# One transfer per piece over all partitions, and three lows made by accumulating DMAs, in a gather and interaction tower

## What is computed

```python
# e: (512, 39, 16), gathered by ids from 39 tables; x0 = xk = e
for W, b in ((w0, b0), (w1, b1), (w2, b2)):         # 128 outputs each
    z = relu(einsum('bhd,bkd,hks->bsd', x0, xk, W) + b)
    xk, direct = z[:, :64], z[:, 64:]               # the last layer: all of z is direct
logit = concat(direct).sum(-1)                      # (512, 256)
h = relu(concat([logit, dense_ctx]) @ W_top1 + b_top1)
h = relu(h @ W_top2 + b_top2)
y = h @ W_top3
```

## Time and profile before

| | us |
|---|---|
| median of 3 runs | 657.21 |
| the runs | 656.03 to 660.27 |
| the profiled execution | 660.38 |
| its span | 658.6 |

### The profile page before, as it was taken

One profiled execution on the slowest core, in us unless ns is written; L12 is line 12 of the kernel. 1 busy time (PEld: TensorE's weight loads), 2 busy tenths in 40 slices (PEclk: granted clock), 3 DMA queues, 4 the chain that ended last, 5 costly groups with the idle time before them and its releaser, 6 DMA issues.

```text
span 658.6 us, 6385 instructions
## 1 busy us (share of the span) xinstructions
PE 613.0 (93%) x1996; PEld 378.3 (57%) x1996; DVE 546.7 (83%) x616; ACT 410.6 (62%) x553; POOL 536.2 (81%) x325
## 2 busy tenths in 40 slices
PE   0169899999999999999999999999999999999998
PEld 0026465666656566656666666666566666655563
DVE  1248699898989898998989898989989898969740
ACT  2025857676676758576766757586777667575622
POOL 6657899898989899998989998999989886747520
PEclk9998899999999999999999999999999999999899
DMA  6689794938374756749384747567494847420000
GB/s 220 136 191 187 160 172 98 180 73 184 89 147 109 139 104 132 148 101 179 71 165 107 146 100 140 114 126 154 95 180 75 162 110 134 96 46 1 0 0 0
DMA packets 53216, 78.60 MB, mean 119 GB/s; under 512 B 39081, under 2 KB 42025, under 8 KB 49891
## 3 DMA queue, kind: packets, MB, share of 16 engines
q1 hardware_dynamic: 47566, 75.11, 54.9%
q0 software_dynamic: 5120, 1.29, 2.0%
q10 hardware_dynamic: 496, 1.80, 1.1%
HBM read 76.23 MB, written 1.94 MB: 119 GB/s over the span
## 4 chain that ended last, share of the span: by engine, by line
PE 38%; POOL 38%; ACT 11%; issue 6%; DMA 4%; DVE 3%; SPq 1%; DVEq 0%; ACTq 0%
POOL low L361 29%; PE z L681 20%; PE z L698 9%; POOL gat L351 9%; ACT x L448 7%; PE z L713 6%; ACT high L428 2%; DMA spread<-x_rows 2%; DVE prod L591 2%; DMA gat<-table_dram,index 2%; ACT r L472 1%; DMA x_rows<-gat 1%; DVE base L626 1%; DVE low L634 1%; PE base L758 1%
## 5 line engine op out<-in xcount | busy, mean ns | idle before, releaser
L361 POOL TENSOR_TENSOR low<-prod,high 128x1024 fp32r<-128x1024 f32 (+2 forms) x160 | 380.7, 2399 | 58.8 <-ACT high L428 57.7
L591 DVE TENSOR_TENSOR prod<-spread,x 128x1024 f32<-128x1024 f32 (+1 forms) x256 | 307.6, 1212 | 38.7 <-ACT x L448 37.7
L681 PE MATMUL z<-prod,w_sb 128*128 128x512 f32 (+3 forms) x608 | 294.0, 604 | 36.9 <-DVE prod L572 32.4
L428 ACT ACTIVATE high<-prod 128x1024 fp32r<-128x1024 f32 (+2 forms) x160 | 167.7, 1058 | 116.9 <-DVE prod L591 98.4
L698 PE MATMUL z<-high,high_w_L 128*128 128x512 f32 (+1 forms) x448 | 205.9, 459 | 1.0 <-ACT high L438 1.0
L713 PE MATMUL z<-low,high_w_L 128*128 128x512 f32 (+1 forms) x448 | 182.6, 488 | 5.5 <-POOL low L361 3.5
L681 PEld LDWEIGHTS z<-prod,w_sb 128*128 128x128 f32 (+3 forms) x608 | 116.2, 192 | 124.0 <-issue 101.6
L351 POOL DMA_INDIRECT gat<-table_dram,index x160 | 154.7, 967 | 37.0 <-issue 35.3
L698 PE MATMUL z<-high,low_w_L 128*128 128x512 f32 (+1 forms) x448 | 179.0, 400 | 0.0
L448 ACT ACTIVATE x<-z,bias_sb 64x512 f32<-64x512 f32 (+1 forms) x186 | 120.2, 646 | 15.1 <-PE z L681 7.4
L713 PEld LDWEIGHTS z<-low,high_w_L 128*128 128x128 f32 (+1 forms) x448 | 82.8, 190 | 71.7 <-issue 45.8
(11 more groups left out here) (37 smaller groups left out, 62.4 us busy)
## 6 DMA issues: line engine op xcount, KB each, us to landing
spread<-x_rows SPq DMA_DIRECT2D x139, 192.0 KB, 13.5
spread<-x_rows SPq DMA_DIRECT2D x30, 546.0 KB
spread<-x_rows SPq DMA_DIRECT2D x47, 256.0 KB, 4.2
spread<-x_rows SPq DMA_DIRECT2D x15, 468.0 KB
x0base<-x_rows SPq DMA_DIRECT2D x47, 78.0 KB
gat<-table_dram,index POOLq DMA_INDIRECT x160, 5.6
x_rows<-gat SPq DMA_DIRECT2D x16, 72.0 KB, 2.2
wt_sb<-wt_dram SPq DMA_DIRECT2D x2, 512.0 KB, 19.0
```

Source lines behind the costliest of these rows:

```text
L361: pool.tensor_tensor(low[0:rows, h, 0:k, :], prod[0:rows, slot(c, kind, g), 0:k, :], high[0:rows, h, 0:k, :].bitcast(F32), ALU.subtract).t ...
L428: act.activation(high[0:rows, split_slot(c, kind, g), 0:k, :], prod[0:rows, slot(c, kind, g), 0:k, :], ACT.Copy).then_inc(high_ready, 1)
L591: dve.tensor_tensor(prod[0:rows, slot(c, kind, g), :, :], spread[0:rows, c % 2, g, :].unsqueeze(1).to_broadcast([rows, k, N]), x[0:rows, : ...
L681: last = pe.matmul(z[:, :], w[0:rows, at + j, :], prod[0:rows, slot(c, kind, g), j, :], start=g == 0 and j == 0, stop=closes and j == k - 1)
```

## The change

Three things are changed.

**Loads.** `load_base` and `load_spread0` issue one DMA over 117 partitions instead of three over 39, and `load_spread` one over 128 partitions for each piece instead of four over 32; the source is given as three blocks of 39 rows, or as four blocks whose row is read 32 times. ACT issues none any more. `ROWS` grows, so that the last rows that are read exist.

**Lows by DMA.** For L2 group 0 and L1 groups 1 and 5 (`BY_DMA`) ACT writes the high with its sign turned, the weights that go with it are turned as well, and a DMA of POOL's queue adds the product onto the high, in place, once PE has summed the high (`add_low`). What stands there then is the low; PE multiplies it by an unturned copy of the high weights (`plus_w`) four groups later (`DMA_PLACES`), or at the end of the stage. POOL's subtraction for these three groups goes. The rings become nine, six and four (`RING`, `HRING`, `LRING`).

**Dense weights.** They lie in `spread0` and are loaded at the end of SP's list, after L0 of the last chunk.

```diff
+ROWS = F + FPT * (-(-max(DPT * T0 - 1, FPT * -(-F // FPT) - F) // FPT))
-RING = 8
-HRING = 4
+RING = 9
+HRING = 6
+LRING = 4
+BY_DMA = (("L2", 0), ("L1", 1), ("L1", 5))
+ADD_PLACES = 1
+DMA_PLACES = 4
...
-                for j in js:
-                    sp.dma_start(x0base[j * F:(j + 1) * F, :], bass.AP(row.tensor, row.offset, [[N, F], [1, N]])
-                                 ).then_inc(base_in, 16)
+                sp.dma_start(x0base[:, :], bass.AP(row.tensor, row.offset, [[0, DPT], [N, F], [1, N]])
+                             ).then_inc(base_in, 16)
...
-                for j in js:
-                    many = min(end, DELTAS - j * T0) - at
-                    row = x0_dram[c, j * T0 + at:j * T0 + at + 1, 0:1]
-                    src = bass.AP(row.tensor, row.offset, [[N, F], [1, many * N]])
-                    sp.dma_start(spread0[j * F:(j + 1) * F, at:at + many, :].rearrange("p t n -> p (t n)"), src
-                                 ).then_inc(done, 16)
+                row = x0_dram[c, at:at + 1, 0:1]
+                src = bass.AP(row.tensor, row.offset, [[T0 * N, DPT], [N, F], [1, (end - at) * N]])
+                sp.dma_start(spread0[0:R0, at:end, :].rearrange("p t n -> p (t n)"), src).then_inc(done, 16)
...
-                for q in qs:
-                    many = min(end, F - q * G1) - at
-                    row = x0_dram[c, q * G1 + at:q * G1 + at + 1, 0:1]
-                    src = bass.AP(row.tensor, row.offset, [[0, QUAD], [1, many * N]])
-                    sp.dma_start(spread[q * QUAD:(q + 1) * QUAD, c % 2, at:at + many, :].rearrange("p g n -> p (g n)"),
-                                 src).then_inc(spread_in[p][c % 2], 16)
+                row = x0_dram[c, at:at + 1, 0:1]
+                src = bass.AP(row.tensor, row.offset, [[G1 * N, FPT], [0, QUAD], [1, (end - at) * N]])
+                sp.dma_start(spread[:, c % 2, at:end, :].rearrange("p g n -> p (g n)"), src
+                             ).then_inc(spread_in[p][c % 2], 16)
...
+            sp.wait_ge(prod_done, PROD_NUMBER[NCH - 1, "L0", G0 - 1])
+            sp.dma_start(wt1_sb, wt1[0:2 * P, :].rearrange("(t p) n -> p t n", p=P)).then_inc(top_in, 16)
...
+            def add_low(c, kind, g):
+
+                n = BY_DMA.index((kind, g))
+                pool.wait_ge(high_summed[n], c + 1)
+                rows, k = shape_of(kind, g)
+                pool.dma_start(high[0:rows, split_slot(c, kind, g), 0:k, :].rearrange("p k n -> p (k n)"),
+                               prod[0:rows, slot(c, kind, g), 0:k, :].rearrange("p k n -> p (k n)"), accum_op=ALU.add
+                               ).then_inc(dma_low[n], 16)
...
+                        for f in gs:
+                            if (kind, f) in BY_DMA and f + ADD_PLACES == g:
+                                add_low(c, kind, f)
...
-            act.wait_ge(base_in, 16 * DPT * (c + 1))
+            act.wait_ge(base_in, 16 * (c + 1))
...
-                               prod[0:rows, slot(c, kind, g), 0:k, :], ACT.Copy).then_inc(high_ready, 1)
+                               prod[0:rows, slot(c, kind, g), 0:k, :], ACT.Copy,
+                               scale=-1.0 if (kind, g) in BY_DMA else 1.0).then_inc(high_ready, 1)
...
+            for n, (kind, g) in enumerate(BY_DMA):
+                at = 2 * SPLIT[kind].index(g)
+                act.activation(plus_w[:, 2 * n:2 * n + 2, :], high_w[kind][:, at:at + 2, :], ACT.Copy
+                               ).then_inc(plus_w_ready, 1)
+            act.wait_ge(plus_w_ready, len(BY_DMA))
+            for kind, g in BY_DMA:
+                at = 2 * SPLIT[kind].index(g)
+                for w in (high_w, low_w):
+                    act.activation(w[kind][:, at:at + 2, :], w[kind][:, at:at + 2, :], ACT.Copy, scale=-1.0
+                                   ).then_inc(signs_turned, 1)
...
-                if old in POOL_NUMBER:
-                    dve.wait_ge(pool_low, POOL_NUMBER[old])
+                if old in TT_NUMBER:
+                    dve.wait_ge(pool_low, TT_NUMBER[old])
+                elif old[1:] in BY_DMA:
+                    dve.wait_ge(dma_low[BY_DMA.index(old[1:])], 16 * (old[0] + 1))
...
+                if by_dma:
+                    n = BY_DMA.index((kind, g))
+                    pe.wait_ge(dma_low[n], 16 * (c + 1))
...
+                    if by_dma:
+                        last = pe.matmul(z[:, :], plus_w[0:rows, 2 * n + j, :], high[0:rows, split_slot(c, kind, g), j, :],
+                                         start=False, stop=closes and j == k - 1)
```

More of the change, by code:

```diff
@@ L74, in stages_of, with places_of, lows_behind @@
     return out
+def places_of(kind, g):
+    return DMA_PLACES if (kind, g) in BY_DMA else 1
+def lows_behind(kind, gs, g):
+    return [f for f in gs if f in SPLIT[kind] and min(f + places_of(kind, f), gs[-1]) == g]
 def finish_order(kind, gs):
@@ L82, in finish_order @@
             out.append(g)
[L83 to L86, removed]
+        out += lows_behind(kind, gs, g)
     return out
@@ L96 @@
 POOL_NUMBER = {x: n + 1 for n, x in enumerate(x for x in SPLITS if x[1:] not in THROUGH_PSUM)}
+LOWS = [x for x in SPLITS if x[1:] not in BY_DMA]
+LOW_NUMBER = {x: n + 1 for n, x in enumerate(LOWS)}
+TT_NUMBER = {x: n + 1 for n, x in enumerate(x for x in LOWS if x[1:] not in THROUGH_PSUM)}
 TILED_NUMBER = {x: n + 1 for n, x in enumerate(x for x in SPLITS if x[1:] in THROUGH_PSUM)}
@@ L193, in tower_kernel @@
         y_sb = sb("y_sb", [1, B])
-        h1 = spread0[:, 0:H1 // P, :]
-        h2 = spread0[:, H1 // P:H1 // P + H2 // P, :]
+        wt1_sb = spread0[:, 0:2, :]
+        wt1c_sb = spread0[0:DENSE, 2, :]
+        ctx_sb = spread0[0:DENSE, 3, :]
+        wt2_sb = spread0[:, 4:6, :].rearrange("p a (b n) -> p (a b) n", n=H2)
+        h1 = spread[:, 0, 0:H1 // P, :]
+        h2 = spread[:, 0, H1 // P:H1 // P + H2 // P, :]
         base = psum("base", [P, N])
@@ L225, in tower_kernel @@
         pool_low = sem("pool_low")
+        dma_low = [sem(f"dma_low_{k}_{g}") for k, g in BY_DMA]
+        high_summed = [sem(f"high_summed_{k}_{g}") for k, g in BY_DMA]
+        plus_w_ready = sem("plus_w_ready")
+        signs_turned = sem("signs_turned")
         tile_prod = sem("tile_prod")
@@ L312, in _ @@
             store_x0(0)
-            load_base(0, (0, 1))
+            load_base(0)
             for n, (at, end) in enumerate(FIRST_CUTS):
-                load_spread0(0, at, end, spread0_first[n], (0, 1))
+                load_spread0(0, at, end, spread0_first[n])
             for p in range(len(PIECES)):
-                load_spread(0, p, (0, 1))
+                load_spread(0, p)
             store_x0(1)
@@ L697, in sum_high @@
                     for v in (high_w, low_w):
-                        pe.matmul(z[:, :], v[kind][0:rows, at + j, :], high[0:rows, h, j, :],
+                        last = pe.matmul(z[:, :], v[kind][0:rows, at + j, :], high[0:rows, h, j, :],
                                   start=g == 0 and j == 0 and v is high_w, stop=False)
+                if (kind, g) in BY_DMA:
+                    last.then_inc(high_summed[BY_DMA.index((kind, g))], 1)
             def sum_low(c, kind, g, closes):
@@ L712, in sum_low @@
                         pe.wait_ge(tile_low, 2 * (tiled - 1) + j + 1)
-                    last = pe.matmul(z[:, :], high_w[kind][0:rows, at + j, :], low[0:rows, h, j, :],
-                                     start=False, stop=closes and j == k - 1)
+                    if by_dma:
+                        last = pe.matmul(z[:, :], plus_w[0:rows, 2 * n + j, :], high[0:rows, split_slot(c, kind, g), j, :],
+                                         start=False, stop=closes and j == k - 1)
+                    else:
+                        last = pe.matmul(z[:, :], high_w[kind][0:rows, at + j, :], low[0:rows, low_slot(c, kind, g), j, :],
+                                         start=False, stop=closes and j == k - 1)
                 last.then_inc(mm_done, 1)
@@ L726, in sum_stage @@
                         sum_whole(c, kind, g, DONE[c, kind, g] == closing)
-                    if g - 1 in gs and g - 1 in SPLIT[kind]:
-                        sum_low(c, kind, g - 1, DONE[c, kind, g - 1] == closing)
-                if gs[-1] in SPLIT[kind]:
-                    sum_low(c, kind, gs[-1], DONE[c, kind, gs[-1]] == closing)
+                    for f in lows_behind(kind, gs, g):
+                        sum_low(c, kind, f, DONE[c, kind, f] == closing)
             pe.wait_ge(w1_in, 32)
```

78 lines of the change are left out of this document (30 added, 48 removed).

## The result

| | before | after |
|---|---|---|
| median of the runs, us | 658.0 (4 runs) | 1101.57 (4 runs) |
| the runs | 656.03 to 660.27 | 1098.69 to 1104.43 |
| the profiled execution | 660.38 | 1100.62 |

The account below looks back on a forecast made before the run. PE bounded the kernel before; the narrow DMA queue would bound it after. Chunk 0's last piece at 89.1 us, 15 x 73.6 and 61.4 remaining sum to 1254.5; less 3.2, forecast 1252 us, range 1000 to 1600.

Parts of the forecast that it names:

- 15 periods: Chunks after the first: each takes 64.7 + 4 + 4.9 = 73.6 us for loads, gap and adds.
- Number of engines: Merged loads: divisor of both sides' outermost counts, so four engines for each piece, three for base and spread0.
- Loads of the busiest engine, 64.7 us: Per chunk the busiest DMA engine moves 1,294 KB at 20 GB/s, longer than the 36.36 us period.
- Gap of 4 us: Between chunks in SP's queue, base waits for the store behind the pieces: 4 us a chunk (3 to 5).
- Adds, 4.9 us a period: Three accumulating transfers beside the loads, 98.3 KB an engine, read and written at 20 GB/s, half beside the gap.
- rival 3: Wide loads, but adds land late: 3 us of PE lost per add, 144 us, total 800 us; chance 0.05.
- Three subtractions go: worth nothing: POOL loses 48 instructions, 115 us, but does not bound a period, so nothing is gained.
- Half clock, compute and the rest covered: PE's 36.36 us compute, half-clock cost of about 3.5 us and further add lateness hide inside the wait for data.
- Rivals 1 and 2: Narrow loads at 12.4 GB/s, 2055 us, chance 0.07; wide hidden loads with adds on time, about 652 us, chance 0.06.
- rival 2: Destination count alone decides, loads run wide and hidden, adds on time: about 652 us, chance 0.06.
- Signs: Expected: about 44,000 packets, period 58 to 95 us, PE share 49%, DVE load waits, mean DMA share 0.2 to 0.3.
- Shared ports: Pieces' partitions 0 to 63 share eight ports: 13.6 GB/s an engine, period about 83 us, time about 1400.

Follow-up runs that it names:

- e2: Kernel after with no adds by DMA (POOL subtracts all ten lows again), merged loads kept: 1001.6 us.
- e1: Kernel after with the loads apart again, all issued from SP's queue, and the three adds kept: 841.5 us.
- e5: Kernel after with the two outer source steps of the merged loads exchanged, three adds kept; output not the reference's: 782.5 us.
- e7: Kernel after with loads apart and only L2 group 0's low added by DMA: 790.1 us.
- e8: Kernel after with loads apart and only L1 group 5's low added by DMA: 686.6 us.
- e9: Kernel after with loads apart and only L1 group 5's low added by DMA, issued one group later in POOL's queue: 665.3 us.
- e6: Kernel after with the two outer source steps of the merged loads exchanged and no adds; output not the reference's: 656.5 us.
- e10: Kernel after with loads apart and no adds, keeping the longer rings and the dense weights in spread0: 657.3 us.

## Why the prediction was right, and where its terms were off

The end, by the prediction's own sum. In the kernel after, the last piece of chunk 0 has landed at 83.81 us (DVE's first L1 group 6) and that of chunk 15 at 1038.68:

```profile
83.81 0.69 DVE L646 TENSOR_TENSOR base<-spread,x 128x512 f32<-128x512 f32 x1 [7.88 <-DMA spread<-x_rows]
...
1038.68 0.69 DVE L646 TENSOR_TENSOR base<-spread,x 128x512 f32<-128x512 f32 x1 [6.16 <-DMA spread<-x_rows]
```

| term | predicted | measured |
|---|---|---|
| last piece of chunk 0 | 89.1 | 83.8 |
| 15 periods | 15 x 73.6 = 1104 | 954.9 = 15 x 63.7 |
| from there to the end of the execution | 61.4 | 1100.6 - 1038.7 = 61.9 |
| sum | 1254.5 | 1100.6 |

- **Number of engines.** Right, and it decides the loads' 344 us: 43,958 packets, and 656.5 us without adds when the source's steps are exchanged. Counting closing packets in the kernel before gave 16 and 13; that unlike sides share a divisor was argued there, and the result bears it out, except that the source's count alone would have given the same.
- **Loads of the busiest engine, 64.7 us.** This is the term that was mis-sized. The bytes stand, the rate doesn't: 20 GB/s was taken, between 12.4 and 24.4. By the records of packets in five periods of e2, the mean packet takes 0.102 us for 2,048 B, 0.265 for 6,144, 0.340 for 8,192 and 0.553 for 14,336. The busiest engine's 39, 64, 32 and 39 of them are 53.4 us a chunk, 1,294 / 53.4 = 24.2 GB/s; this is the prediction's own fast bound (53.0 at 24.4). The error is 11.3 us a period, 170 us in all, and with 53.0 in place of 64.7 the sum would have been about 1067. What had slowed the loads before was absent once four engines ran.
- **Gap of 4 us.** Right. In e2 no load is under way for 3.6 us of a period (its window of 424 to 427 us above has a DMA share of 0.05), and 53.4 + 3.6 = 57.0 of its 57.24. That SP would be held for 22 us in an issue was not foreseen, but it adds nothing: the pieces run on meanwhile.
- **Adds, 4.9 us a period.** Near: 62.99 - 57.24 = 5.75 over the five periods shown of each, and (1101.6 - 1001.6) / 15 = 6.7 over the whole. But the words around it, that lateness is covered by the wait for data, hold only because the loads were slower. With loads at their old pace the adds cost 184 us (e1). That was rival 3, given 0.05 and 800 us: the mechanism was real. Its price of 3 us an add was 3.8 on the mean in e1 (184 / 48) and 2.6 in e5 (126 / 48, 782.5 us), which is rival 3 as it was put, one wide transfer for each piece; and PE's wait for a DMA falls on one add in three. The prediction's argument for keeping it small, four groups' time of 6.5 us, failed against a landing of up to 13.5 us beside the loads (e7).
- **Three subtractions go: worth nothing.** Right, and less than nothing with loads apart. POOL stands in front of the adds (255.5 us in e1, 205.1 in after) for more than the 115 us removed, though much of this is PE's own lateness; the prediction named the wait for PE's matmuls but not what stands behind it in POOL's queue. In e8 it alone costs about 21 us, which is what e9 gets back.
- **Half clock, compute and the rest covered.** Right: PE's busy time grew by 114 us and the sum needs none of it.
- **Rivals 1 and 2.** At 12.4 GB/s (2055 us) nothing ran; the loads of rival 2, wide and hidden, are those of e6 (656.5 us, without adds); its adds on time did not come true, as e5 shows.
- **Signs.** The packets came as said, and the period of 63.0 lies in 58 to 95. DVE's waits for loads came too, but the list names a transfer for only a part of them (66.4, 34.2 and 30.7 us in all); the 21 us a chunk before spread0's products stand under "issue". PE's share was to be 49% and is 66%, for the shorter span and the lower clock; the mean DMA share was to be 0.2 to 0.3 and is 0.36 in a period. Here the sign didn't follow from the prediction's own terms: 4.5 MB of loads at 20 GB/s and 9.8 us an engine for the adds are 0.33 of 16 engines in 73.6 us. The adds themselves were not slower than taken: by the records of packets 0.34 us for 4,096 B, 8.2 us a chunk for the 98.3 KB of an engine, of which about 6 lengthen the period.
- **Shared ports.** From what the Trainium skill says of shared ports (SBUF — State Buffer, "Door 1: The DMA port swizzle") the prediction estimated 13.6 GB/s for each of two engines in step, and a time of about 1400. e2's window shows 25 on the four, so no such slowing is seen here; whether two engines ever were on one port at once, no view shows.

## What to carry to other kernels

Merging several DMAs into one changes how the work is divided: look at the outermost counts of both sides, since an outer step of 3 or 4 in the source left 3 or 4 of the 16 engines here, and a mean DMA share of 0.36 hides that they are full. Putting the larger count outermost cost nothing and, for base and spread0 with the weights laid out to match, kept the merge (658.7 us against 794.4); but the merge gained nothing over separate transfers. A DMA that stands in for an engine's work must be timed against the loads issued just before it and issued where nothing is queued behind its wait; otherwise it can cost more than the instruction it saves, as here.

## What was not expected of the hardware

- A single DMA engine ran the loads at about 24 to 25 GB/s when four did them (e2), and at 12.4 when up to sixteen read the same rows for neighbouring partitions. By one measure for all, the bytes of q1 over the time of its packets, it is 22.3 GB/s in e2, 13.0 in e10 with loads apart, and 19.8 in e6, where sixteen engines work with the source's steps exchanged (79.23 MB in 38.1% of 654.9 us). Four engines thus carried more than half of what sixteen carried (101 GB/s against 182).
- The issue of a small store took SP 22.13 us while the loads ahead of it were running on few engines, and a wait for a load can be shown as "issue".
- An accumulating transfer of 512 KB from SBUF to SBUF landed after 4.7 to 5.6 us at the median (e9, after), and 13.5 us passed from its issue to the matmul that waited for it where base, spread0 and two pieces were being issued from 7 us before to 2 us behind it (e7).
- Parts that cost 344 and 184 us alone cost 444 together, and a part that looks free behind another (adds, 100 us on top of 1001.6) isn't once the other is mended.
